# A routed feed-forward, a recurrent mix and the feed-forward again, on one core: new tables for the planner, four gather buffers, seven last steps combined by matrices, and memsets between the last gathers

## The reference

```python
x = x + 0.5 * ffn(layernorm(x), gate_w, w1, w3, w2)
x = x + attention(layernorm(x), ...)      # a recurrence over time, WKV
x = x + 0.5 * ffn(layernorm(x), gate_w, w1, w3, w2)
```

## Time and profile before

| | |
|---|---|
| median of 3 runs | 606.3 us (605.97 to 606.87) |
| the profiled execution | 611.62 us, its span 609.8 us |
| PE busy | 525.3 us (86%) |
| DVE busy | 438.5 us (72%) |
| POOL busy | 398.1 us (65%) |
| ACT busy | 318.7 us (52%) |
| POOL, pace memsets (L801) | 232, 133.0 us |
| POOL waiting for slots (L766 <- DVE slot) | 157.6 us, 8 times |

### The profile page before, as it was taken

The page is one execution under the profiler, slowest core; times in us unless marked ns, Lnnn a source line. Parts: engine busy times, 40 slices in busy tenths (PEclk is TensorE's granted clock), DMA queues, the critical chain, the costliest instruction groups (busy, mean ns, idle before and its releaser), DMA issues.

```text
span 609.8 us, 18683 instructions
## 1 busy us (share of the span) xinstructions
PE 525.3 (86%) x5906; PEld 480.7 (79%) x5906; DVE 438.5 (72%) x1241; ACT 318.7 (52%) x703; POOL 398.1 (65%) x500
## 2 busy tenths in 40 slices
PE   1234899999999899999989989999999999998992
PEld 1233789998977789778888779898798988998981
DVE  4871873556778998879999885887888857248742
ACT  5433574444675657576375663587456454443420
POOL 1182049499999991199954999300985997999982
PEclk9999899999999999999999998999999999999997
DMA  8963233445332221222221132210112432523322
GB/s 278 330 210 110 60 102 110 131 145 128 90 98 83 72 79 55 69 62 66 83 76 49 59 114 75 67 42 27 54 59 84 113 107 76 182 81 102 97 71 60
DMA packets 88632, 60.28 MB, mean 99 GB/s; under 512 B 10337, under 2 KB 82146, under 8 KB 88418
## 3 DMA queue, kind: packets, MB, share of 16 engines
q1 hardware_dynamic: 55586, 31.03, 17.3%
q0 software_dynamic: 8192, 16.79, 9.6%
q10 hardware_dynamic: 24768, 11.28, 6.4%
HBM read 29.69 MB, written 29.37 MB: 97 GB/s over the span
## 4 chain that ended last, share of the span: by engine, by line
PE 61%; issue 10%; ACT 9%; DVE 8%; SPq 5%; POOL 4%; DMA 1%; another core or an unknown queue 1%; DVEq 0%; ACTq 0%; POOLq 0%
PE py L1330 20%; PE pa L1316 16%; PE pb L1316 15%; PE pT L1303 3%; POOL rows_in L766 3%; PE bkB L1380 2%; ACT xn L866 2%; PE bkB L1401 2%; DVE h L1170 1%; ACT sil L847 1%; POOL pace L801 1%; SPq L664 1%; PE bkA L1380 1%; SPq L677 1%
## 5 line engine op out<-in xcount | busy, mean ns | idle before, releaser
L766 POOL DMA_INDIRECT rows_in<-parts,slot x128 | 135.2, 1057 | 179.5 <-DVE slot L1091 157.6
L1330 PE MATMUL py<-ffn_w,h 128*128 x1416 | 196.6, 282 | 9.5 <-ACT yrow L830 8.1
L1170 DVE TENSOR_TENSOR h<-sil,pb 128x512 f32<-128x512 f32 x177 | 120.8, 686 | 107.1 <-PE pb L1316 56.3
L1330 PEld LDWEIGHTS py<-ffn_w,h 128*128 128x128 f32 x1416 | 173.2, 193 | 15.1 <-issue 12.3
L1316 PE MATMUL pa<-rT,ffn_w 128*128 128x128 f16 (+1 forms) x1752 | 150.9, 232 | 18.1 <-DVE h L1170 9.8
L1316 PE MATMUL pb<-rT,ffn_w 128*128 128x128 f16 (+1 forms) x1752 | 155.8, 231 | 0.0
L1316 PEld LDWEIGHTS pa<-rT,ffn_w 128*128 x1752 | 123.3, 99 | 33.4 <-issue 21.8
L785 POOL DMA_INDIRECT yg<-rows_out,slot x120 | 121.0, 1008 | 19.4 <-issue 19.2
L801 POOL MEMSET pace<- 128x544 uint8 x232 | 133.0, 573 | 0.2
L1316 PEld LDWEIGHTS pb<-rT,ffn_w 128*128 x1752 | 122.9, 98 | 7.5 <-issue 0.2
L847 ACT ACTIVATE sil<-pa 128x512 f32<-128x512 f32 x177 | 105.4, 595 | 37.8 <-PE pa L1316 32.3
(11 more groups left out here) (167 smaller groups left out, 493.5 us busy)
## 6 DMA issues: line engine op xcount, KB each, us to landing
rows_out<-yrow ACTq DMA_DIRECT2D x162, 64.0 KB
rin<-rows_in SPq DMA_DIRECT2D x65, 128.0 KB
rows_in<-zrow SPq DMA_DIRECT2D x34, 128.0 KB
shared<-in_w SPq DMA_DIRECT2D x16, 256.0 KB, 6.8
rin<-rows_in SPq DMA_DIRECT2D x47, 64.0 KB
rows_in<-zrow SPq DMA_DIRECT2D x2, 1472.0 KB, 12.1
xres<-in_x SPq DMA_DIRECT2D x4, 512.0 KB, 5.8
ffn_w<-in_w SPq DMA_DIRECT2D x8, 256.0 KB
```

Source lines behind the costliest of these rows:

```text
L766: pool.indirect_dma_start(rows_in[g][:], bass.IndirectOffsetOnAxis(ap=slot[:, c, at:at + 1], axis=0), parts[:, at, :], None).then_inc(s_sc ...
L1170: dve.tensor_tensor(h[:, t % RING, :], sil[:, t % 2, :], pb[t % 2][:], ALU.mult).then_inc(s_h, 1)
L1330: mm = pe.matmul(py[:], h[:, step % RING, at:at + T], w, start=(c == 0), stop=(c == FC - 1))
```

## The change

`LATE` goes from 5 to 7: the last seven tiles go by matrices, and `rows_last` ends two tiles earlier. The parts of the matrices (three for each tile, `HOT_PARTS`) no longer follow each tile from a fixed one on, but those at least 8 tiles after `weights8.0` with less than 1.5 us of planned VectorE work; parts that find no tile are done at the start of `combine_last`. `GSLOTS` goes from 3 to 4. `SLIP` and `SPACE` are larger, and `DUE_SHIFT` and `NOT_BEFORE` are new tables. A memset to `pace` now also stands between the last eight gathers (the condition before the other memsets was always met).

```diff
-LATE = 5
+LATE = 7
-HOT_AT = TILES - 3 * LATE - 4
+HOT_PARTS = 3
-GSLOTS = 3
+GSLOTS = 4
-SLIP = {"dve": 6.2, "act": 2.6, "pe": 2.0}
-SPACE = 1.6
+SLIP = {"dve": 6.8, "act": 2.8, "pe": 2.0}
+SPACE = 1.7
 DUE_SHIFT = {
-    "stats6.1": -4, "combine2.0": -2, "stats5.0": 30
+    "combine2.1": -12, "pick6.0": 18, "combine1.1": 37, "stats7.0": 41, "pick4.0": 50, "stats6.1": 52,
+    "stats6.0": 72, "stats5.0": 76, "stats3.0": 90, "stats3.1": 104
 }
 NOT_BEFORE = {
...
-    "att2.1": 106, "combine3.0": 106, "mstats3.0": 107, "combine3.1": 112, "count6.0": 118, "turn_m3.1": 121,
-    "peak3.1": 126, "r3.1": 127, "exps3.1": 129, "scatter7.0": 133, "divide3.1": 134, "divide23.1": 135,
-    "stats8.0": 138, "turn8.0": 142, "combine4.1": 148, "combine5.0": 163
...
+    79, "combine2.0": 81, "out1.1": 82, "mstats2.0": 85, "norm5.1": 86, "hi_m2.0": 89, "mrsqrt2.1": 90,
+    "scatter5.0": 92, "pk2.1": 97, "att2.0": 100, "weigh2.1": 103, "add2.0": 105, "divide2.1": 105,
+    "combine3.0": 109, "mstats3.0": 110, "hi6.0": 111, "mrsqrt3.0": 111, "hi6.1": 113, "peak3.0": 117,
+    "weigh3.0": 121, "divide3.0": 122, "xT3.1": 123, "exps3.1": 129, "sum_b3.1": 132, "scatter7.0": 133,
+    "rsqrt8.0": 145, "combine5.0": 158, "combine6.0": 173
 }
...
+ROUTED = next(p[0] for p in PLAN if p[1:] == ("weights", LAST, 0))
+LOADED = {t: sum(WORK["dve"].get(p[1], 0.0) for p in PLAN if p[0] == t) for t in range(TILES)}
+HOT_TILES = [t for t in range(ROUTED + 8, TILES) if LOADED[t] < 1.5][:HOT_PARTS * LATE]
...
-                if t < TILES - 1:
-                    wait(pool, s_pace, sent - PACES + 1)
-                    pool.memset(pace[:, sent % PACES, :], 0).then_inc(s_pace, 1)
+                wait(pool, s_pace, sent - PACES + 1)
+                pool.memset(pace[:, sent % PACES, :], 0).then_inc(s_pace, 1)
             for run in range(RUNS):
                 for one in every(run, range(UNITS[run] if PEND[run] == TILES else 0)):
                     gather(*one)
+                    sent += 1
+                    if one != (run, UNITS[run] - 1, JU - 1, TOPK - 1):
+                        wait(pool, s_pace, sent - PACES + 1)
+                        pool.memset(pace[:, sent % PACES, :], 0).then_inc(s_pace, 1)
...
-                if HOT_AT <= t < HOT_AT + 3 * LATE:
-                    one_hot(*divmod(t - HOT_AT, 3))
+                if t in HOT_TILES:
+                    one_hot(*divmod(HOT_TILES.index(t), HOT_PARTS))
...
                 slot_ = (len(GATHERS) - 1) % GSLOTS
+                for n in range(len(HOT_TILES), HOT_PARTS * LATE):
+                    one_hot(*divmod(n, HOT_PARTS))
                 for j in range(JU):
```

More of the change, by code:

```diff
@@ L712, in spread_route @@
             def spread_route(t):
-                made = next(p[0] for p in PLAN if p[1:] == ("weights", LAST, 0))
-                assert made + 8 <= HOT_AT
-                if t == made + 1:
+                if t == ROUTED + 1:
                     sp.wait_ge(s_route, 1)
                     sp.dma_start(route_last, route[:].rearrange("p q j -> p (q j)")).then_inc(s_bounce, 16)
-                if t == made + 4:
+                if t == ROUTED + 4:
                     sp.wait_ge(s_bounce, 16)
```

## The result

The changed kernel takes 610.55 us (609.85 to 611.6), the kernel before 606.87 in the same comparison: a ratio of 1.0064, 95% interval 1.005 to 1.0077. It is 3.7 us slower, where 604.2 and a gain were forecast (610.55 lies inside the forecast's widest range, 599.0 to 611.0, but on the other side of before). The profiled execution took 610.55 as well, its span 608.5. The profile of before that the prediction was made against is one of the longer executions (611.62). Spans are some 2 us shorter than the times.

A forecast was written before the change was run, and what follows sets the result against it. GpSimd was taken to bound the end once ScalarE's 6.38 us wait is gone. GpSimd's line (602.06 + 3.1 + 1.1 - 2.5 - 1.5) and VectorE's both end at 603.3, 2.1 before 605.40: 606.3 - 2.1 = 604.2 us, range 599.0 to 611.0.

The forecast's parts named there:

- The end of the span: Tail: GpSimd's last gather lands at 602.06, VectorE's last pair starts about 604.36, so GpSimd has 2.3 us to spare.
- The memsets: Between the last eight gathers: seven more memsets add 0.44 us each, together +3.1 us on GpSimd's line.
- Four buffers: GpSimd before run 8's scatters: reordering removes 2.47 us of idle time, -2.5 us (bounds -2.5 and 0).
- The tables: VectorE work moves from before 375 us into the looser stretch after: -1.5 us on both lines (bounds -5.4, +3.0).
- rival A: Middle, 195 to 375 us: tables give a third of TensorE's idle time, -5.4 for -1.5; 600.3 us, chance 0.17.
- The matrices: Tail: 14 of 21 parts placed, seven left, VectorE done with them at 600.5; end 604.8 in place of 605.40.
- the prediction's other term: GpSimd's gathers beside the matrices' products on VectorE: four more are slowed, +1.1 us on GpSimd's line (0 to 1.6).
- B: GpSimd's line alone decides, tables give nothing; holds once the last landing is later than 604.36; 608.2 us, chance 0.16.
- C: Run 8's rows come at 549.3, 2.8 us after TensorE's turn at 546.54; 608.5 us, chance 0.17.
- The marks: Signs in the trace; forecast wrong if tile 130's h moves over 3 us or ScalarE's long wait before the last copy stays.

The follow-up runs named there:

- 610 level: The kernel before at the slower of its two levels across comparisons, 609.6 to 610.4 us; the other is 606.6 to 607.0 us.
- the control: The kernel before, unchanged, run again for a second trace: 606.78 us beside 606.76, ratio 1.0006.
- e15: The kernel before with only the seven memsets between the last eight gathers added, second run on another chip: ratio 1.0052, 3.2 us.
- e2: The kernel before with only the seven memsets between the last eight gathers added: 610.61 us, ratio 1.0065.
- run 8: Not an experiment: the kernel's last run, with eight scatters on GpSimd; TensorE turned its first tile at 546.54 us in the profile of before.
- e11: The kernel before with only GSLOTS = 4: 610.31 us, ratio 0.9994.
- e5: The kernel before with only the new tables, SLIP and SPACE: 609.18 us beside 607.0, ratio 1.0046.
- e16: The changed kernel without the last seven memsets, three gathers moved ahead of run 8's scatters: 604.7 us beside 606.62 for the kernel before, ratio 0.9973.
- run 7: Not an experiment: a run within the kernel; its first scatter is the 177th of GpSimd's 256 transfers and starts at 459.03 us in the control.
- e3: The changed kernel with LATE = 5 in place of 7, no left-over products in the tail: 611.57 us, ratio 1.0081 to the kernel before.

## Why the prediction was wrong, by its steps

*The end of the span: the step that failed.* "GpSimd has 2.3 us to spare in this execution" compared its last landing with VectorE's last pair. The span doesn't end by either. It ends when GpSimd's DRAIN is over, 9.45 us after its last instruction, in every trace whose GpSimd is that late, and in the profile of before GpSimd was already the bound (600.35 + 9.45 = 609.8, VectorE's 605.40 + 2.0 = 607.4). The spare time was on VectorE's side, 2.4 us. So the sum should have been a sum over GpSimd's line alone, and its last instruction, 600.35, should have been moved by every term in full. The chain of waits could not show it, but the rows did hold a warning: 4.4 us behind a last add which only waited for ScalarE. A second fault of the base: that profile was like those of the 610 level, so the 6.38 us of ScalarE and the 2.47 of GpSimd were not those of the executions that the forecast's 606.3 came from (2.40 and 1.02 in the control).

*The memsets.* +3.1 forecast, 3.0 in the groups, 3.2 (e15) and 3.8 (e2) timed. Right in size; they were set against spare time that GpSimd did not have.

*Four buffers.* The 2.47 us of idle time before run 8's scatters were to go, -2.5. They became 4.45. Against the control, where it was 1.02, this is +3.4 us, the largest term (the 2.47 to 3.30 of the old order are from the 610 level, so they are not the measure here). The step took for granted that the planner would use the fourth buffer to reorder; it changed nothing (e11). The longer idle time came with the new tables (e5), and three transfers moved by hand remove it (e16).

*The tables.* -1.5 was taken with -5.4 as the bound. At run 7's scatters the gain was 4.05 us, nearer to rival A. It reached the end only in part, and only once the order was right.

*The matrices.* Forecast: 14 of 21 parts placed, seven at the end, VectorE done at 600.5. `weights8.0` came to tile 150, 15 found a place, and VectorE was done with the rest at 593.9, mostly because its last combine began at 585.72 and not at 591.44; not a bound. What they did was on GpSimd's line, as the prediction's other term had it (+1.1, measured 1.5 in the last eight and 0.5 just before). The gather at 588.19 lasted 1.81 beside the product at 588.07, one undisturbed 0.95; of the 13 gathers that overlap such a product after, 7 took over 1.1. Here the trace goes on speaking against the inference of the Trainium skill (SBUF — State Buffer, "Who interferes with whom") that such a product does not stall descriptor generation. But e3, which has no such overlap in the last eight gathers, was not faster, so the term alone was not shown in a time.

*The rivals.* B, "GpSimd's line alone decides", named the right mechanism and gave 608.2. It lacked the idle time, and it put the point from which the line decides at a last landing at 604.36 when in that profile it decided always. C named run 8's rows, for the right reason that run 8's routing is late; but TensorE did not wait for them (the turn at 542.20 has no wait); GpSimd waited for the slots and VectorE for the spread route. Rival A's gain and B's loss both happened, in one kernel. That 610.55 lies in the range is luck: no rival's sum gives it, and the upper end was C's with one more tile (which is 608.5 + 3.0 = 611.5, not 611.0).

*The marks.* Memsets 1.7 us apart: yes (596.42, 598.09). Last gather generated before 601: yes, 599.04, and the time was slow nonetheless, which is the failed step again. No idle time of GpSimd after run 7's scatters: no, 4.45. VectorE from the last combine into products: yes (588.07), and six left-over parts for about seven. The sign of B, a last landing that VectorE's last pair waits for, was there (0.92). Tile 130's h moved by 8.0 us against the profile of before (463.63 to 455.63) and by 4.0 against the control, both over the 3 that were named as a sign of a wrong forecast. ScalarE's long wait did not come again, but neither is it in the control: this says nothing of the memsets.

## What to carry to other kernels

Before trusting the chain of waits for the end of a span, look for the closing instructions of each engine (here under the line that opens the kernel), and tabulate for each engine how far its last instruction stands from the end over two or three traces; the engine with the constant distance is the bound. Before building a sum on a profile, see whether its execution is one of the usual length. An idle time that one part of a change is meant to remove can be made again, larger, by another part: follow each queue written in a fixed order past the moved steps and ask whether its head is ready when its turn comes. A spacing between transfers that looks like pure cost in one comparison should be tried in several, on several chips, before it is taken out.

## What was not expected of the hardware

- GpSimd's closing DRAIN ended 9.22 to 9.24 us after its last instruction in all 20 traces, be that an indirect DMA (594.82 to 604.05) or a memset (599.36 to 608.60); with the exchange of semaphores the span ended 9.45 us after it.
- Indirect gathers issued 1.25 us apart, 20 in a row, held ScalarE and then TensorE up by some 16 us in two comparisons on two chips (ratios 1.038 and 1.042) and not at all in a third (0.99). With full memsets between them, starts 1.69 us apart, no such wait was seen.
- Beside a VectorE product of 1.1 us with two operands in SBUF, a gather's generation took up to 1.81 us for 0.95, but only about half of the gathers so placed were slowed (5 of 10 before, 7 of 13 after).
- TensorE's granted clock fell to 0.71 over 4 us at run 5's start in e2 and stayed at 1.00 in the control, for the same code up to there, which goes with about 1 us.
